# Moving the second gate's beta product and the query products from VectorE to GpSimd, and splitting the prediction's matmuls around U

## The chip, the core and the metric

The kernel runs on one core of a Trainium2 chip. The metric is the device time of one execution in microseconds, from the hardware; what is shown is the median over runs. Engines are named as in the profile: PE is TensorE's matmul, DVE is VectorE, ACT is ScalarE, POOL is GpSimd, SP is SyncE.

## The reference

The layer is an attention block with two recurrent states, followed by a routed feed-forward block. With 2 sequences of 2048 tokens, 16 heads and head size 64, each token does, per head:

```python
pred = einsum(S, kn);  r = clip(v_t - pred, -1, 1)
S = a_t * S;  S = S + b_t * kn (x) (v_t - kn.S)
o = einsum(S, q_t)
R = aR_t * R; R = R + g_t * kn (x) (r - kn.R)
o = o + einsum(R, q_t)
```

Here `b_t` is the first gate's beta and `g_t` the second gate's (it scales the whole update of R). The output is projected, normalised and added; then 64 experts (8 for each token) and one shared expert follow, with another layernorm and residual.

## The kernel before

The program has a short first stage, then `attention`, a loop over 32 chunks of 64 tokens, then a stage that runs the experts over 320 tiles of 128 tokens, then a last stage of layernorms. Each engine has its own hand-written program inside a stage; the order in the source is the order on the engine, and semaphores tie the engines together. Work for the next chunk (its projections, gates and keys) is done inside the loop body of the present one under `if front`.

In a chunk the recurrence is turned into triangular systems of 64 tokens. The tiles that matter:

- `S`, `R` are the states; `pq[:, 0]` are keys with the decay of the steps before them, `pq[:, 1]` and `rqplus` are queries times decays for the first and second state; `dec` (the tile `z`) holds the decays, `c` their inverses; `kplus`, and `c` again, are the scaled keys.
- `L_s`, `L_r` hold the triangles that are inverted: GpSimd makes beta times the strict mask (`row_coefficients`), VectorE multiplies it into PE's product in `masked`. The inverse of the 32x32 diagonal blocks is made on VectorE in 30 steps, and leaves it as `N` and `T`, two transposes that are the last things of a long unbroken VectorE run.
- PE then makes `Z` and `X` (the off-diagonal blocks), ACT and POOL put the blocks together in `inv_s` and `inv_r`. POOL copies the diagonal blocks of `inv_r`, ACT its off-diagonal ones.
- PE makes `U` = inv_s times B, then `PR` (the prediction: `pq[:,0]` with S plus `pqT` with U), `SU` (update of S), `NS` (norms of the next keys), the first part of `O`, `SD` (shared expert), `W` = inv_r times `BR`, the rest of `O`, `RU` (update of R), the next chunk's triangles `A`, `OUT` and `V`.
- VectorE makes `BR` from PR: subtract, clip, subtract `KRt`, multiply by the second gate's beta. Then come the keys of the next chunk (`k`, `c`, `kplus`, `pq`), the add into S, the query products, the add into R, and `masked`.

Matmul results go through six banks in turn (`SMALL`, in the order of `order_of_jobs`): a product waits until the one six places before it has been emptied. `O_begun` says that PE has done the first part of `O`, which reads the old query products; `queries_made` says that the new ones are there, and ACT and PE wait for it in the next chunk. POOL also issues eight scatters of rows per chunk (L391) from the third chunk on, numbers 5 to 7 of them behind `BR_ready` and `O_begun`.

## Time and profile before

| what | value |
|---|---|
| median of 3 runs | 3480.25 us (3474.77 to 3484.2) |
| the profiled execution | 3481.59 us, its span 3479.8 us |
| mean granted TensorE clock over the span | 0.889 |
| chunk loop, first to last N transpose | 110.0 to 2537.0 us |

The chunk loop takes some seventy per cent of the time, the expert stage nearly all of the rest. A busy share is an average over these stages. A line number in a row is a line of the kernel before; a pair such as `BR<-BR,beta` is the tile written and the tiles read.

### The profile page before, as it was taken

What the parts mean: (1) busy time and instruction counts of PE and PEld (TensorE: products, weight loads), DVE (VectorE), ACT (ScalarE), POOL (GpSimd) and SP (SyncE); (2) the same over time, 40 slices, a digit from 0 to 9 for tenths busy, and PEclk for the clock granted to TensorE, in tenths of its full rate; (3) what the DMA queues carried; (4) which work ended last, traced back from release to release, by engine and by line L of the source; (5) the groups of instructions that cost most, each with busy time, mean ns of one, the idle gap of its engine ahead of it and who ended that gap; (6) DMA issues with size and microseconds to landing.
All of it is one profiled execution on the core that took longest, in us unless ns stands there. A gap on an engine that the chain in (4) does not pass through costs nothing. (4 is left out here: it accounts for less than half of the span.)

```text
span 3479.8 us, 135741 instructions
## 1 busy us (share of the span) xinstructions
PE 2906.5 (84%) x56922; PEld 2571.7 (74%) x56922; DVE 2644.2 (76%) x6931; ACT 1948.5 (56%) x5132; POOL 1229.9 (35%) x1001
## 2 busy tenths in 40 slices
PE   4888888888888888889988888888855998889980
PEld 4888887878888887878888887888744776667760
...
DMA packets 193480, 240.15 MB, mean 69 GB/s; under 512 B 26738, under 2 KB 171251, under 8 KB 192115
## 3 DMA queue, kind: packets, MB, share of 16 engines
...
## 5 line engine op out<-in xcount | busy, mean ns | idle before, releaser
L391 POOL DMA_INDIRECT table<-xrow,place_i x256 | 280.4, 1095 | 764.0 <-DVE BR L866 237.8
L1475 PE MATMUL bank<-w,route 128*128 x2560 | 370.8, 288 | 35.7 <-issue 12.2
L1105 POOL COPY inv_r<-N 32x512 f32<-32x512 f32 x128 | 136.4, 1065 | 736.5 <-DVE N L842 732.5
L1475 PEld LDWEIGHTS bank<-w,route 128*128 128x128 f32 x2560 | 311.9, 192 | 104.2 <-issue 101.2
L457 DVE TENSOR_TENSOR tri<-tri,step 128x58 f32<-128x58 f32 (+13 forms) x896 | 305.5, 341 | 30.8
L456 DVE TENSOR_TENSOR step<-tri 128x58 f32<-128x58 f32 (+13 forms) x896 | 301.7, 337 | 26.4
L1490 PE MATMUL bank<-w,seen 128*128 x640 | 215.0, 418 | 52.5 <-DVE y L1563 10.2
L1551 DVE COPY to_row<-shared 128x1 int32<-128x1 int32 x228 | 35.1, 154 | 269.1 <-DMA acc<-sh_h,to_row 43.3
L1082 POOL COPY T<-L_s 32x512 f32<-32x512 f32 x64 | 38.7, 605 | 359.5 <-DVE L_s L778 358.2
L1490 PEld LDWEIGHTS bank<-w,seen 128*128 128x128 f32 x640 | 95.8, 189 | 89.2 <-issue 83.8
L589 PE MATMUL bank<-B,kT_r 64*64 64x64 f32 x2048 | 110.4, 300 | 61.4 <-DVE S L883 61.4
L783 DVE TENSOR_TENSOR_SCAN c<-restart,z 128x1024 f32<-128x1024 bf16 x62 | 158.3, 2592 | 0.0
L589 PEld LDWEIGHTS bank<-B,kT_r 64*64 64x64 f32 x2048 | 105.1, 210 | 65.6 <-DVE S L883 65.6
L948 ACT ACTIVATE z<-bank,neg_bias 128x128 f32<-128x128 f32 x496 | 137.6, 373 | 28.5 <-PE bank L604 26.1
L566 PE MATMUL bank<-S,pq 64*64 64x64 f32 x2048 | 109.6, 311 | 44.1 <-ACT U L924 44.1
L1518 ACT COPY route<-bank 128x256 f32<-128x256 f32 x320 | 119.5, 374 | 46.4 <-PE bank L1460 46.4
L1551 DVE COPY to_row<-xrow 128x1 int32<-128x1 int32 x92 | 14.2, 154 | 169.9 <-ACT shared L1527 62.6
L604 PE MATMUL bank<-xnT,wa 128*128 128x128 f32 x992 | 126.7, 289 | 18.7 <-ACT xnT L984 18.7
L969 ACT ACTIVATE S<-S,dec_end 128x64 f32<-128x64 f32 x512 | 125.8, 334 | 26.8 <-DVE S L883 26.7
L604 PEld LDWEIGHTS bank<-xnT,wa 128*128 128x128 f32 x992 | 120.8, 202 | 22.9 <-ACT xnT L984 22.8
L699 PE MATMUL bank<-Z,T 32*32 32x32 f32 x4096 | 119.8, 235 | 20.6 <-issue 20.0
L928 ACT COPY k<-bank 128x512 f32<-128x512 f32 x62 | 36.3, 585 | 179.3 <-PE bank L604 179.3
...
## 6 DMA issues: line engine op xcount, KB each, us to landing
table<-blank SPq DMA_DIRECT2D x320, 129.0 KB
...
```

The lines of the kernel that those rows point to most:

```text
L391: nc.gpsimd.indirect_dma_start(out=table, out_offset=bass.IndirectOffsetOnAxis(ap=t.place8_i[:, k:k + 1], axis=0), in_=row[:, :], in_offse ...
L456: link(nc.vector.tensor_tensor(step, s[:, 0:k, k:k + 1].broadcast_to([P, k, rest]), over(s[:, k, k + 1:Q], k), ALU.mult))
L457: link(nc.vector.tensor_tensor(s[:, 0:k, k + 1:Q], s[:, 0:k, k + 1:Q], step, ALU.add))
L589: mm = nc.tensor.matmul(ps[r, C * i:C * i + C], lhsT(r, u), rhs(r, u), start=(m == 0), stop=(m == len(pairs) - 1))
L604: mm = nc.tensor.matmul(ps[:, P * m:P * m + P], w[:, kt, P * hp:P * hp + P], t.xnT[:, kt, :], start=(kt == 0), stop=(kt == 1))
L699: mm = nc.tensor.matmul(ps[top, Q * u:Q * u + Q], t.T[top, 16 * g + u, :], t.Z[top, 16 * g + u, :], start=True, stop=True)
L783: nc.vector.tensor_tensor_scan(t.c[:, gate, :, :].rearrange("p u n -> p (u n)"), t.restart[:], t.z[:, gate, :], 0.0, ALU.mult, ALU.add).th ...
L948: ins = nc.scalar.activation(t.z[:, gate, P * hp:P * hp + P], ps[:, P * m:P * m + P], ACT.Exp, bias=t.neg_bias[:, gate, hp:hp + 1], scale= ...
L969: ins = nc.scalar.activation(state[:, u, :], state[:, u, :], ACT.Copy, scale=t.dec_end[n % 2][:, g, u:u + 1])
L1105: ins = nc.gpsimd.tensor_copy(t.inv[1][r, :, Q * (q % 2):Q * (q % 2) + Q], t.N[r, 16:32, :])
L1475: mm = nc.tensor.matmul(ps[:, begin:begin + n], t.xT_slot[i % 3][:, P * kt:P * kt + P], weights(i, 257 * kt + begin, n), start=(kt == 0), ...
L1490: nc.tensor.matmul(t.ps[y_bank[i % 2]][:, 0:256], t.hT_slot[i % 3][:, :], weights(i, 514, 256), start=True, stop=True).then_inc(t.sem["y_d ...
```

## The change

The second gate's beta no longer multiplies `BR` on VectorE. It multiplies `inv_r` on POOL: the four diagonal copies become products with beta, two more products scale the off-diagonal blocks once ACT has put them there, and the making of `L_s` and `L_r` is split around these. The two query products and the copy of the last decays go from VectorE to POOL, behind scatters 5 and 6 and the wait for `O_begun`, ahead of scatter 7. On PE the half of PR that reads S is issued before U, into its own banks, and the half that reads U after it; PR has a semaphore of its own, `PR_done`, and takes the two bank turns before U's.

```diff
@@ -72,7 +72,7 @@
     jobs = [("XT", "")] * front + two("KS") + two("a") * front + two("KR") + two("r") * front + [("BG", "")] * front
     jobs += [("RT", "")] + [("PQ", str(i)) for i in range(4)] + two("k") * front + [("RL", "")] + two("RQ")
     jobs += [("KT", f"{g}{h}") for g in range(2) for h in range(2)] + two("q") * front + [("SG", "")]
-    jobs += two("Z") + two("X") + two("U") + two("PR") + two("SU") + two("NS") * front + two("O") + [("SD", "")]
+    jobs += two("Z") + two("X") + two("PR") + two("U") + two("SU") + two("NS") * front + two("O") + [("SD", "")]
     jobs += two("W") + two("RU") + ends + [("RK", "")] * route + [("OUT", "")] + two("V") * front
     return jobs
 
...
@@ -88,7 +88,7 @@
             signalled = 0
             for p, (n, kind, name) in enumerate(mine):
                 seen[table[kind]] += 1
-                signalled += kind != "O"
+                signalled += kind not in ("O", "PR")
                 self.engine[n, name] = ("" if table is SMALL else "front_", table[kind])
                 self.done[n, name] = (p, signalled)
                 self.before[n, name] = (mine[p - banks][0], mine[p - banks][2]) if p >= banks else None
...
@@ -491,9 +491,9 @@
     return nc.scalar.activation(t.bgz[:].rearrange("p g u -> p (g u)"), ps[:, 0:32], ACT.Exp, scale=-1.0)
 
 
-def row_coefficients(nc, t, beta):
-
-    for g, h in STREAMS:
+def row_coefficients(nc, t, beta, streams):
+
+    for g, h in streams:
         half = slice(8 * h, 8 * h + 8)
         nc.gpsimd.tensor_tensor(t.L[g][:, half, :], bc(beta[:, g, half], C), over(t.neg_strict[:], 8),
                                 ALU.mult).then_inc(t.sem["coef_ready"], 1)
...
@@ -699,13 +699,15 @@
                             mm = nc.tensor.matmul(ps[top, Q * u:Q * u + Q], t.T[top, 16 * g + u, :],
                                                   t.Z[top, 16 * g + u, :], start=True, stop=True)
                     mm.then_inc(t.sem["mm_done"], 1)
+                PR = [begin(n, "PR0"), begin(n, "PR1")]
+                four(PR, odd_unit, [(lambda r, u: t.pq[r, 0, u, :], of(t.S))], last=False, whole=True)
                 pe.wait_ge(t.sem["B_ready"], n + 1)
                 wait_emptied(pe, t, o, n, "X0")
                 pe.wait_ge(t.sem["inv_s_ready"], n + 1)
                 crossed(n, "U", [(of(t.inv[0]), of(t.B))])
                 wait_emptied(pe, t, o, n, "U1")
-                crossed(n, "PR", [(lambda r, u: t.pq[r, 0, u, :], of(t.S)),
-                                  (lambda r, u: t.pqT[r, u, 0, :], of(t.U))])
+                for ins in four(PR, odd_unit, [(lambda r, u: t.pqT[r, u, 0, :], of(t.U))], first=False, whole=True):
+                    ins.then_inc(t.sem["PR_done"], 1)
                 for h in range(2):
                     units(n, f"SU{h}", h, [(of(t.kT[0]), of(t.U))])
                 if front:
...
@@ -720,7 +722,6 @@
                 ps = begin(n, "SD")
                 wait_emptied(pe, t, o, n, "SG")
                 shared_down(nc, t, ps).then_inc(t.sem["front_mm"], 1)
-                wait_emptied(pe, t, o, n, "X1")
                 pe.wait_ge(t.sem["inv_r_ready"], n + 1)
                 pe.wait_ge(t.sem["BR_ready"], 2 * n + 2)
                 crossed(n, "W", [(of(t.inv[1]), of(t.BR))])
...
@@ -856,14 +857,14 @@
                     route_best(nc, t, link)
                 for h in range(2):
                     r, rest = even_odd(t.BR, h), even_odd(t.KRt, h)
-                    ps = mm(n, f"PR{h}")
+                    dve.wait_ge(t.sem["PR_done"], 2 * n + h + 1)
+                    ps = o.bank(t, n, f"PR{h}")
                     nc.vector.tensor_tensor(r, even_odd(t.V, h), blk(ps[:, :]),
                                             ALU.subtract).then_inc(t.sem["dve_emptied"], 1)
                     wait_emptied(dve, t, o, n, f"PR{h}")
                     link(nc.vector.tensor_scalar(r, r, -1.0, 1.0, ALU.max, ALU.min))
                     wait_emptied(dve, t, o, n, "KR1")
-                    link(nc.vector.tensor_tensor(r, r, rest, ALU.subtract))
-                    nc.vector.tensor_tensor(r, r, bc(t.beta[n % 2][:, 1, h:16:2], C), ALU.mult).then_inc(t.sem["BR_ready"], 1)
+                    nc.vector.tensor_tensor(r, r, rest, ALU.subtract).then_inc(t.sem["BR_ready"], 1)
                 if route:
                     dve.wait_ge(t.sem["sel_ready"], o.base("sel_ready", n + 1))
                     route_weights(nc, t, link, t.xrow[n % 2])
...
@@ -882,11 +883,6 @@
                     ps = mm(n, f"SU{h}")
                     nc.vector.tensor_tensor(t.S[:, half[h], :], blk(ps[:, :]), t.S[:, half[h], :],
                                             ALU.add).then_inc(t.sem["dve_emptied"], 1)
-                if front:
-                    wait_emptied(dve, t, o, n, "q1")
-                    nc.vector.tensor_tensor(t.pq[:, 1, :, :], t.q[:], t.dec[:, 0, :, :], ALU.mult)
-                    nc.vector.tensor_tensor(t.rqplus[:], t.q[:], t.dec[:, 1, :, :], ALU.mult)
-                    nc.vector.tensor_copy(t.dec_end[(n + 1) % 2][:], t.dec[:, :, :, C - 1]).then_inc(t.sem["queries_made"], 1)
                 for h in range(2):
                     ps = mm(n, f"RU{h}")
                     nc.vector.tensor_tensor(t.R[:, half[h], :], blk(ps[:, :]), t.R[:, half[h], :],
...
@@ -1102,22 +1098,41 @@
                 pool.wait_ge(t.sem["N_ready"], n + 1)
                 for q in range(4):
                     r = slice(Q * q, Q * q + Q)
-                    ins = nc.gpsimd.tensor_copy(t.inv[1][r, :, Q * (q % 2):Q * (q % 2) + Q], t.N[r, 16:32, :])
+                    ins = nc.gpsimd.tensor_tensor(t.inv[1][r, :, Q * (q % 2):Q * (q % 2) + Q], t.N[r, 16:32, :],
+                                                  bc(t.beta[n % 2][r, 1, :], Q), ALU.mult)
+                ins.then_inc(t.sem["inv_r_begun"], 1)
+                pool.wait_ge(t.sem["inv_r_begun"], n + 1)
+                if front:
+                    wait_done(pool, t, o, n, "Z1")
+                    pool.wait_ge(t.sem["beta_ready"], n + 1)
+                    row_coefficients(nc, t, t.beta[(n + 1) % 2], STREAMS[0:2])
+                    pool.wait_ge(t.sem["coef_ready"], o.base("coef_ready", n) + 2)
+                wait_emptied(pool, t, o, n, "X1")
+                for j in range(2):
+                    r = slice(C * j, C * j + Q)
+                    ins = nc.gpsimd.tensor_tensor(t.inv[1][r, :, Q:2 * Q], t.inv[1][r, :, Q:2 * Q],
+                                                  bc(t.beta[n % 2][r, 1, :], Q), ALU.mult)
                 ins.then_inc(t.sem["inv_r_ready"], 1)
                 pool.wait_ge(t.sem["inv_r_ready"], n + 1)
                 if front:
-                    wait_done(pool, t, o, n, "Z1")
-                    pool.wait_ge(t.sem["beta_ready"], n + 1)
-                    row_coefficients(nc, t, t.beta[(n + 1) % 2])
+                    row_coefficients(nc, t, t.beta[(n + 1) % 2], STREAMS[2:4])
                 if n >= 2:
                     pool.wait_ge(t.sem["BR_ready"], 2 * n + 1)
                     scatter_row(nc, t, d.table, t.xrow[(n - 1) % 2], 5)
                     pool.wait_ge(t.sem["BR_ready"], 2 * n + 2)
                     scatter_row(nc, t, d.table, t.xrow[(n - 1) % 2], 6)
+                if front:
+                    pool.wait_ge(t.sem["dec_ready"], 2 * n + 2)
+                    wait_emptied(pool, t, o, n, "q1")
                     pool.wait_ge(t.sem["O_begun"], n + 1)
+                    nc.gpsimd.tensor_tensor(t.pq[:, 1, :, :], t.q[:], t.dec[:, 0, :, :], ALU.mult)
+                    nc.gpsimd.tensor_tensor(t.rqplus[:], t.q[:], t.dec[:, 1, :, :], ALU.mult)
+                    nc.gpsimd.tensor_copy(t.dec_end[(n + 1) % 2][:], t.dec[:, :, :, C - 1]).then_inc(t.sem["queries_made"], 1)
+                if n >= 2:
                     scatter_row(nc, t, d.table, t.xrow[(n - 1) % 2], 7)
                     wait_scattered(pool, t, n - 1)
                 if front:
+                    pool.wait_ge(t.sem["queries_made"], o.base("queries_made", n) + 1)
                     diagonal(n)
 
 
...
@@ -1169,7 +1184,7 @@
                                     t.k[:].rearrange("p u n -> p (u n)"), ALU.mult).then_inc(t.sem["keys_squared"], 1)
             pool.wait_ge(t.sem["beta_ready"], 1)
             pool.wait_ge(t.sem["late_loaded"], 16 * len(late))
-            row_coefficients(nc, t, t.beta[0])
+            row_coefficients(nc, t, t.beta[0], STREAMS)
             pool.wait_ge(t.sem["key_ready"], 1)
             for g in range(2):
                 pool.wait_ge(t.sem["dec_ready"], g + 1)
```

On VectorE, in one chunk, this is what stood from the scaling of the next keys by their norms to the triangles (`x2` is a pair of equal instructions):

```order
L873 TENSOR_TENSOR k<-k,tri 128x1024
L876 TENSOR_TENSOR c<-k,c 128x2048
L877 TENSOR_TENSOR kplus<-k,z 128x2048
L878 TENSOR_TENSOR pq<-k,z 128x16x63
L879 COPY pq<-k 128x16
L883 TENSOR_TENSOR S<-bank,S 128x512 x2
L887 TENSOR_TENSOR pq<-q,z 128x1024
L888 TENSOR_TENSOR rqplus<-q,z 128x1024
L889 COPY dec_end<-z 128x32
L892 TENSOR_TENSOR R<-bank,R 128x512 x2
L778 TENSOR_TENSOR L_s<-bank,L_s 128x8x64 x2
```

and this is what stands there now, with the lines' new numbers:

```order
L874 TENSOR_TENSOR k<-k,tri 128x1024
L877 TENSOR_TENSOR c<-k,c 128x2048
L878 TENSOR_TENSOR kplus<-k,z 128x2048
L879 TENSOR_TENSOR pq<-k,z 128x16x63
L880 COPY pq<-k 128x16
L884 TENSOR_TENSOR S<-bank,S 128x512 x2
L888 TENSOR_TENSOR R<-bank,R 128x512 x2
L779 TENSOR_TENSOR L_s<-bank,L_s 128x8x64 x2
```

The three instructions on queries and decays are gone; keys, S, R and the triangles keep their order. Ahead of this piece the two products `BR<-BR,beta` are gone as well.

On POOL one chunk, from the transposed inverse to the copies of the triangles' diagonals, read before:

```order
L1105 COPY inv_r<-N 32x16x32 x4
L498 TENSOR_TENSOR L_s<-beta,neg_strict 128x512 x2
L498 TENSOR_TENSOR L_r<-beta,neg_strict 128x512 x2
L391 DMA table<-xrow,place_i 41088x258 x3
L1082 COPY T<-L_s 32x512 x2
L1082 COPY T<-L_r 32x512 x2
```

and reads now:

```order
L1101 TENSOR_TENSOR inv_r<-N,beta 32x16x32 x4
L498 TENSOR_TENSOR L_s<-beta,neg_strict 128x512 x2
L1113 TENSOR_TENSOR inv_r<-inv_r,beta 32x16x32 x2
L498 TENSOR_TENSOR L_r<-beta,neg_strict 128x512 x2
L391 DMA table<-xrow,place_i 41088x258 x2
L1128 TENSOR_TENSOR pq<-q,z 128x1024
L1129 TENSOR_TENSOR rqplus<-q,z 128x1024
L1130 COPY dec_end<-z 128x32
L391 DMA table<-xrow,place_i 41088x258
L1078 COPY T<-L_s 32x512 x2
L1078 COPY T<-L_r 32x512 x2
```

The query products stand between scatters 6 and 7, and the diagonal copies `T<-L_s` come behind them.

On PE the piece from the off-diagonal blocks to the update of S, where PR alternated between its two sources in sixteen groups, began before with

```order
L699 MATMUL bank<-Z,T 32x32 x64
L566 MATMUL bank<-B,inv_s 64x64 x32
L566 MATMUL bank<-S,pq 64x64 x4
L566 MATMUL bank<-U,pqT 64x64 x4
L566 MATMUL bank<-S,pq 64x64 x4
```

and reads now

```order
L699 MATMUL bank<-Z,T 32x32 x64
L566 MATMUL bank<-S,pq 64x64 x32
L566 MATMUL bank<-B,inv_s 64x64 x32
L566 MATMUL bank<-U,pqT 64x64 x32
L589 MATMUL bank<-U,kT_s 64x64 x32
```

The S half of PR stands whole ahead of U, the U half whole behind it.

## Rows read from the trace of the kernel before

**Rows 1.** Page, part 1: busy us, share of the span, instructions of each engine
```profile
PE 2906.5 (84%) x56922; PEld 2571.7 (74%) x56922; DVE 2644.2 (76%) x6931; ACT 1948.5 (56%) x5132; POOL 1229.9 (35%) x1001
```
**Rows 2.** One line's instructions: the transpose that ends each chunk's triangle inversion
```profile
L842 DVE STREAM_TRANSPOSE N<-tri x32: 2007/2070/2101, 110.0 to 2537.0; 128x1024 f32<-128x1024 f32 x32
```
**Rows 3.** Timeline of one chunk, DVE: start, duration, line, operation, idle before, releaser
```profile
1222.01 0.69 DVE L860 TENSOR_TENSOR BR<-V,bank 128x512 f32<-128x512 f32 x1 [1.91 <-PE bank L566]
...
1223.92 0.69 DVE L866 TENSOR_TENSOR BR<-BR,beta 128x512 f32<-128x512 f32 x1
...
1229.86 1.23 DVE L873 TENSOR_TENSOR k<-k,tri 128x1024 f32<-128x1024 f32 x1 [1.96 <-ACT tri L472]
1231.12 2.29 DVE L876 TENSOR_TENSOR c<-k,c 128x2048 f32<-128x2048 f32 x1
1233.33 2.28 DVE L877 TENSOR_TENSOR kplus<-k,z 128x2048 f32<-128x2048 f32 x1
1235.53 1.20 DVE L878 TENSOR_TENSOR pq<-k,z 128x1008 f32<-128x1008 f32 x1
...
1236.74 1.28 DVE L883 TENSOR_TENSOR S<-bank,S 128x512 f32<-128x512 f32 x2
1237.93 1.22 DVE L887 TENSOR_TENSOR pq<-q,z 128x1024 f32<-128x1024 f32 x1
1239.07 1.22 DVE L888 TENSOR_TENSOR rqplus<-q,z 128x1024 f32<-128x1024 f32 x1
...
1240.31 1.41 DVE L892 TENSOR_TENSOR R<-bank,R 128x512 f32<-128x512 f32 x2
1242.16 1.29 DVE L778 TENSOR_TENSOR L_s<-bank,L_s 128x512 f32<-128x512 f32 x2 [0.45 <-PE bank L566]
```
**Rows 4.** Timeline of the same chunk, PE
```profile
1214.79 2.27 PE L566 MATMUL bank<-B,inv_s 64*64 64x64 f32 x64
1218.29 0.49 PE L566 MATMUL bank<-S,pq 64*64 64x64 f32 x8 [1.23 <-ACT U L924]
...
1221.75 3.09 PE L589 MATMUL bank<-U,kT_s 64*64 64x64 f32 x64
...
1232.08 1.16 PE L566 MATMUL bank<-BR,inv_r 64*64 64x64 f32 x64
...
1237.48 3.39 PE L589 MATMUL bank<-B,kT_r 64*64 64x64 f32 x62 [1.91 <-DVE S L883]
```
**Rows 5.** Timeline of the same chunk, POOL
```profile
1208.32 4.44 POOL L1105 COPY inv_r<-N 32x512 f32<-32x512 f32 x4 [21.38 <-DVE N L842]
1212.85 3.89 POOL L498 TENSOR_TENSOR L_s<-beta,neg_strict 128x512 f32<-128x512 f32 x2
1216.71 2.04 POOL L498 TENSOR_TENSOR L_r<-beta,neg_strict 128x512 f32<-128x512 f32 x2
...
1231.37 2.90 POOL L391 DMA_INDIRECT table<-xrow,place_i  x1 [3.00 <-PE bank L566]
1243.61 1.25 POOL L1082 COPY T<-L_s 32x512 f32<-32x512 f32 x2 [9.34 <-DVE L_s L778]
```
**Rows 6.** Timeline of the last stage, DVE and POOL, two places
```profile
3432.40 1.22 DVE L1598 TENSOR_TENSOR sum<-sum 128x1024 f32<-128x1024 f32 x1
3432.57 3.25 POOL L1637 TENSOR_TENSOR row<-sum,row 128x1024 f32<-128x1024 f32 x1 [11.66 <-DVE sum L1609]
...
3447.71 2.34 POOL L1637 TENSOR_TENSOR row<-sum,row 128x1024 f32<-128x1024 f32 x1 [1.79 <-DVE sum L1609]
3448.72 2.42 DVE L1598 TENSOR_TENSOR sum<-sum 128x1024 f32<-128x1024 f32 x1 [1.08 <-DMA row<-x_rows]
```
**Rows 7.** Windows, same chunk: length; busy PE, PEld, DVE, ACT, POOL; granted clock; DMA; GB/s
```profile
1237.70:1241.10 3.40, 3.40 (x82) 3.40 (x82) 3.37 (x6) 3.40 (x16) 0.00 (x0) 0.50 0.12 30
```
**Rows 8.** Timeline of three chunks later, DVE
```profile
1470.52 1.28 DVE L883 TENSOR_TENSOR S<-bank,S 128x512 f32<-128x512 f32 x2
...
1475.29 1.28 DVE L778 TENSOR_TENSOR L_s<-bank,L_s 128x512 f32<-128x512 f32 x2
```

2 lines of the change are left out of this document (1 added, 1 removed).

## The prediction

> **What bounds the kernel now.** I read the page first: VectorE is busy 76% of the span and PE 84%, POOL 35% [rows 1]. These shares mix stages, so I read the chunk loop alone. Its transposes of N start at 110.0 and, 32 of them, at 2537.0 [rows 2], so a chunk takes (2537.0 - 110.0)/31 = 78.3 us. Then I read the timelines of one middle chunk, engine by engine, looking for the places where an engine stands idle and who lets it go on.
>
> VectorE runs without a pause from the triangles `L_s` at 1242.16 until the next chunk's prediction PR. It pauses three times: 1.91 us for PR, 1.96 us for ACT's key norms, 0.45 us for PE's triangle products [rows 3]. PE pauses 1.23 us for ACT's copy of U and 1.91 us for VectorE's add into S, which empties the bank that RU needs [rows 4]. So in the part of the chunk that the change touches, the chain that sets the end is: U, copy of U, PR, SU and the norms on PE; norms on ACT; then on VectorE `k`, `c`, `kplus`, `pq`, S (1229.86 to 1238.02); then RU and the triangle products on PE; then `L_s` on VectorE. What matters is which of the edits lies on that chain.
>
> **Beta off VectorE.** Two products of 0.69 us leave [rows 3]. They stand before the 1.96 us wait for the norms, and these come from PE and ACT. W, which reads BR, starts at 1232.08, long after BR is made, with no idle time before it [rows 3, 4]. So VectorE waits 1.4 us longer for the norms: price 0. On POOL four copies become products and two more are added. The nearest rows: the four copies took 4.44 us, two 128x512 products 2.04 us where nothing was in the way and 3.89 us where a scan was [rows 5]. The six products cost thus 6 x 1.02 = 6.1 us to 6 x 1.94 = 11.7 us, in place of 4.44. L_s and L_r cost 5.9 us as before. POOL started at 1208.32; even at the upper end it is through at 1208.3 + 11.7 + 5.9 = 1225.9, and `inv_r` is ready before that, ahead of W at 1232.08. Products on POOL also hold up some of VectorE's short routing operations; the cover is the 1.91 us before PR plus the norm wait of 1.96 + 1.4 us, together 5.3 us. If that cover were gone, each microsecond over it would be one on the chain, 31 us in all.
>
> **PR in two halves.** PE goes from X straight into U, with no idle time [rows 4], so there is no gap for the first half to fill. The whole of PR took from 1218.29 to 1221.75, 3.46 us; half is 1.73 us. U and its copy end 1.73 us later, and 1.73 us less remains behind them: PR ends where it did. Price 0. If the copy's start hid a little of ACT's own work it could be 0.1 us better; if the groups run worse apart than interleaved, worse by as little.
>
> **Query products off VectorE.** 1.22 + 1.22 us and a short copy leave, standing between the add into S and the add into R: from 1237.93 to 1240.31, 2.38 us [rows 3]. It looks like 74 us in 31 chunks. But RU starts at 1237.48, off the first half of S, and takes 3.39 us; the triangles follow it on PE, and `L_s` waited 0.45 us for PE even with the query products in place [rows 3, 4]. VectorE would only wait longer. Price 0 while PE is this slow there. The granted clock in that stretch is 0.50, 1.2 GHz of the two levels [rows 7]. Where it was full, the distance from S to `L_s` was 1475.29 - 1470.52 = 4.77 us against 5.42 us, with no wait [rows 3, 8]; only in such chunks can the removal pay.
>
> **Query products onto POOL.** This is the term that decides. POOL may start when `O_begun` arrives. Before, scatter 7 waited for just that and started at 1231.37 [rows 5]; the query products start there now, 0.25 us after VectorE began `c` at 1231.12. VectorE then does three products with both operands in SBUF: `c`, `kplus`, `pq` [rows 3]. The last stage shows what becomes of two such products on the two engines. POOL's product, started 0.17 us after VectorE's, took 3.25 us and ended 2.20 us after the end of VectorE's; with nothing in the way it took 2.34 us, the same shape as a query product. VectorE's, started 1.01 us into POOL's, took 2.42 in place of 1.22 us and ended 1.08 us after POOL's end, so 0.14 us of its duration passed before it was held up [rows 6]. They take turns, a whole instruction at a time, and each waits for the other.
>
> Turn by turn. `c` ends at 1233.41. POOL's first product has waited since 1231.4, ends at 1233.41 + 2.20 = 1235.61. `kplus` ends at 1235.61 + 2.28 - 0.14 = 1237.75 in place of 1235.61: 2.14 us late. POOL's second, waiting by then, ends at 1239.95; `pq` ends at 1239.95 + 1.20 - 0.14 = 1241.01 in place of 1236.73: 4.28 us late. If POOL comes first, before `c`, two of the three are held up all the same. The adds into S have one operand in PSUM, and a copy on POOL beside the same kind of instruction at 1243.61 took 0.63 us each, so they add nothing. So the add into S is 4.28 us late, on the chain: RU, triangles and `L_s` move by as much, PE standing idle 1.91 + 4.28 = 6.2 us. 31 chunks prepare a next one: 31 x 4.28 = +133 us. Bounds: 0, if POOL's products always yield and run behind `pq`; 2.14 us per chunk if only one finds itself in the way; above, 4.28 and what the clock costs on top (below). I take 4.28, since both directions of the turn have their row. The Trainium skill (Perfetto Trace Analysis, Optimizing Scalar/DVE Operations) says that offloading from a saturated DVE to GpSimd may make sense, but that the two share an SBUF read port, so it might not help. By that sentence alone this term would be 0 or better, and the rows say that it costs.
>
> What is behind POOL's products: scatter 7, then the copies into T. The queries end near 1240.2, `L_s` now comes near 1246.4, so there is room for the scatter (2.90 us at most in these rows) before the copies [rows 5]: price 0.
>
> **Sum.** 3481.6 (the profiled execution) + 133 = 3614.6. That execution is 1.3 us over the median of the runs shown, so 3613 for the median.
>
> **Rivals.** (1) One turn only. Speaks for it: the second product may find `pq` already begun. 31 x 2.14 = 66 us: 3547. A PE clock that recovers earlier, since the S half of PR joins X and U in one unbroken stretch, gives similar: half of SU's 3.09 us would be 1.5 us per chunk, 48 us off the 133: 3565. Against: in the middle chunk nothing but the copy of U separated PR from U before either.
> (2) The clock costs on top. PE idles 6.2 us before RU. RU then runs 3.39 us at the low level, but the triangles ran mostly at full clock, and would slow too: about 2.2 us more at the very most (their share of 5.42 - 3.39 = 2.0 us, doubled), so up to 62 us: 3675; half of that, 3644, is likelier. The Trainium skill (TensorE: Matmul & The Clock Gate, HAM oscillation) says that recurring waits throttle the engine again each time. By that rule this is what would come; the trace agrees as far as the 0.50 in the stretch after a wait of 1.91 us.
> (3) No change: POOL's products yield to VectorE's, which are queued back to back, and run beside the adds. All moved work was hidden or becomes hidden: 3480. Against: POOL's product in the last stage did not yield to what VectorE had next [rows 6], but VectorE's next there was no such product.
> (4) Faster: as (3), and PE, less broken, keeps its full clock over RU. Then VectorE sets `L_s`, and the removed 2.38 us and the 0.65 us between 5.42 and 4.77 pay, less what PE needs: at most 3.03 x 31 = 94 us, I take half: 3433. It decides from the point where the turns cost less than 3.03 us per chunk, so one turn at 2.14 us would already leave it a little faster if the clock held. Against: the low clock stands after the very wait that would have to shrink.
>
> **Chances.** Two full turns, 0.68; (1) 0.12; (2) 0.10; (3) 0.05; (4) 0.05. The range runs from 3545, below both forms of (1), to 3655, above the likelier half of (2). 0.3%, some 10 us, is about what a measurement of this kernel can tell from no change. Faster by more 0.05, within it 0.05, slower 0.90. The forecast's own range, given its case, is 3590 to 3640.
>
> **What the changed profile would show.** Each turn: `kplus` and `pq` at about 4.4 and 3.3 us in place of 2.28 and 1.20, and POOL's two products at over 4 us each in place of 2.33. `k` waits some 3.4 us for the norms. RU waits over 6 us for S. R and `L_s` wait for PE, by more than 0.45 us. The U wait on PE stays near 1.23 us and PR ends at the same distance from N. The forecast is wrong if `kplus` and `pq` keep their durations, or if the long run of VectorE from `L_s` to N changes its length.

## The result and the profile after

The changed kernel takes 3595.97 us (median of 4 runs, 3594.27 to 3598.03) against 3481.61 us before (3474.77 to 3484.2): a ratio of 1.0332, 95% interval 1.0314 to 1.0350. It is 3.3% slower. Its profiled execution took 3595.86 us, with a span of 3594.1 us and a mean granted TensorE clock of 0.889, as before. Comparisons leave disturbed runs out.

Part 1 of its page (busy us, share, instructions), which answers to [rows 1]:

```profile
PE 2875.6 (80%) x56922; PEld 2555.4 (71%) x56922; DVE 2756.1 (77%) x6774; ACT 1951.3 (54%) x5132; POOL 1605.9 (45%) x1158
```

VectorE has 157 instructions less and is busy 112 us more. That is the first thing to see: what was left on it became longer. The transpose that ends each inversion, answering to [rows 2]:

```profile
L843 DVE STREAM_TRANSPOSE N<-tri x32: 2017/2080/2106, 112.2 to 2655.9; 128x1024 f32<-128x1024 f32 x32
```

A chunk takes (2655.9 - 112.2)/31 = 82.05 us in place of 78.29. 31 x 3.76 = 116.7 us, against 114.3 us between the two profiled executions: the loss is in the chunk loop. Timeline of one chunk on DVE (its N starts at 1102.49), answering to [rows 3]:

```profile
1118.43 1.00 DVE L339 TENSOR_TENSOR route<-route 128x64 f32<-128x64 f32 x1
1119.35 0.67 DVE L862 TENSOR_TENSOR BR<-V,bank 128x512 f32<-128x512 f32 x1
...
1123.86 1.23 DVE L874 TENSOR_TENSOR k<-k,tri 128x1024 f32<-128x1024 f32 x1
1125.12 2.29 DVE L877 TENSOR_TENSOR c<-k,c 128x2048 f32<-128x2048 f32 x1
1127.33 4.44 DVE L878 TENSOR_TENSOR kplus<-k,z 128x2048 f32<-128x2048 f32 x1
1131.69 3.34 DVE L879 TENSOR_TENSOR pq<-k,z 128x1008 f32<-128x1008 f32 x1
...
1135.08 1.27 DVE L884 TENSOR_TENSOR S<-bank,S 128x512 f32<-128x512 f32 x2
1137.83 0.69 DVE L888 TENSOR_TENSOR R<-bank,R 128x512 f32<-128x512 f32 x1 [1.48 <-PE bank L589]
1139.54 0.69 DVE L888 TENSOR_TENSOR R<-bank,R 128x512 f32<-128x512 f32 x1 [1.02 <-PE bank L589]
1141.31 1.29 DVE L779 TENSOR_TENSOR L_s<-bank,L_s 128x512 f32<-128x512 f32 x2 [1.08 <-PE bank L566]
```

POOL in the same chunk, answering to [rows 5]:

```profile
1104.77 8.12 POOL L1101 TENSOR_TENSOR inv_r<-N,beta 32x512 f32<-32x512 f32 x4 [21.84 <-DVE N L843]
1112.96 2.05 POOL L498 TENSOR_TENSOR L_s<-beta,neg_strict 128x512 f32<-128x512 f32 x2
1115.09 2.14 POOL L1113 TENSOR_TENSOR inv_r<-inv_r,beta 32x512 f32<-32x512 f32 x2
1117.30 2.04 POOL L498 TENSOR_TENSOR L_r<-beta,neg_strict 128x512 f32<-128x512 f32 x2
...
1126.89 2.73 POOL L1128 TENSOR_TENSOR pq<-q,z 128x1024 f32<-128x1024 f32 x1 [2.64 <-PE bank L566]
1129.57 4.40 POOL L1129 TENSOR_TENSOR rqplus<-q,z 128x1024 f32<-128x1024 f32 x1
1133.92 1.21 POOL L1130 COPY dec_end<-z 128x32 f32<-128x32 f32 x1
```

Read the two timelines against each other. `c` (from 1125.12, 2.29 us) ends at 1127.41, as long as in before. POOL's first product ends at 1129.62, `kplus` at 1131.77, POOL's second at 1133.97, `pq` at 1135.03. The ends alternate, 2.21, 2.15, 2.20 and 1.06 us apart, about what each instruction takes alone, less the overlap with the one before. So each duration in the rows holds the other engine's turn too. From the start of `c` to the add into S it is 1135.08 - 1125.12 = 9.96 us, where it was 1236.74 - 1231.12 = 5.62 us [rows 3].

PE in the same chunk, answering to [rows 4]:

```profile
1113.12 1.57 PE L566 MATMUL bank<-B,inv_s 64*64 64x64 f32 x64
1115.82 1.17 PE L566 MATMUL bank<-U,pqT 64*64 64x64 f32 x63 [1.12 <-ACT U L920]
...
1116.86 1.98 PE L589 MATMUL bank<-U,kT_s 64*64 64x64 f32 x62
...
1135.81 3.57 PE L589 MATMUL bank<-B,kT_r 64*64 64x64 f32 x62 [4.63 <-DVE S L884]
```

RU waits 4.63 us for S, where it waited 1.91. But SU (`U,kT_s`) takes 1.98 us where it took 3.09: the clock is up again by then. Windows (length; busy PE, PEld, DVE, ACT, POOL; clock; DMA; GB/s) show where it rises. First two of the chunk of [rows 4], which hold its U and PR:

```profile
1214.30:1217.70 3.40, 2.75 (x84) 2.40 (x78) 3.23 (x15) 2.79 (x6) 3.40 (x3) 0.50 0.03 7
1217.70:1221.10 3.40, 2.81 (x104) 2.82 (x108) 2.06 (x12) 3.37 (x5) 1.04 (x2) 0.50 0.00 0
```

Then three of the chunk above, in after, the last of which holds the U half of PR:

```profile
1106.70:1110.00 3.30, 2.62 (x94) 2.40 (x90) 3.30 (x2) 3.19 (x7) 3.18 (x3) 0.58 0.18 56
1110.00:1113.50 3.50, 3.50 (x131) 3.44 (x131) 3.43 (x5) 3.02 (x5) 3.42 (x2) 0.50 0.02 5
1113.50:1117.00 3.50, 2.38 (x133) 2.24 (x127) 3.19 (x17) 2.45 (x5) 3.36 (x4) 0.92 0.02 5
```

Three groups of before that the rows ahead of the prediction don't have (busy us, mean ns | idle before them in the whole run, and which instruction ended it):

```profile
L860 DVE TENSOR_TENSOR BR<-V,bank 128x512 f32<-128x512 f32 x64 | 43.8, 684 | 69.8 <-PE bank L566 69.8
...
L873 DVE TENSOR_TENSOR k<-k,tri 128x1024 f32<-128x1024 f32 x31 | 38.0, 1225 | 48.4 <-ACT tri L472 48.4
...
L330 DVE TENSOR_TENSOR route<-route,groups 128x64 f32<-128x64 f32 x32 | 7.2, 226 | 1.1
```

and the groups of after:

```profile
L1129 POOL TENSOR_TENSOR rqplus<-q,z 128x1024 f32<-128x1024 f32 x31 | 130.6, 4212 | 0.0
L878 DVE TENSOR_TENSOR kplus<-k,z 128x2048 f32<-128x2048 f32 x31 | 126.8, 4090 | 0.0
L1128 POOL TENSOR_TENSOR pq<-q,z 128x1024 f32<-128x1024 f32 x31 | 112.1, 3617 | 82.9 <-PE bank L566 82.9
L879 DVE TENSOR_TENSOR pq<-k,z 128x1008 f32<-128x1008 f32 x31 | 95.2, 3070 | 0.0
L888 DVE TENSOR_TENSOR R<-bank,R 128x512 f32<-128x512 f32 x64 | 44.3, 691 | 79.2 <-PE bank L589 79.2
L862 DVE TENSOR_TENSOR BR<-V,bank 128x512 f32<-128x512 f32 x64 | 43.3, 677 | 9.5 <-PE bank L566 9.5
L779 DVE TENSOR_TENSOR L_s<-bank,L_s 128x512 f32<-128x512 f32 x64 | 41.2, 686 | 48.5 <-PE bank L566 48.5
L874 DVE TENSOR_TENSOR k<-k,tri 128x1024 f32<-128x1024 f32 x31 | 38.0, 1225 | 22.6 <-ACT tri L472 21.5 <-DVE xrow L347 0.2
L330 DVE TENSOR_TENSOR route<-route,groups 128x64 f32<-128x64 f32 x32 | 33.1, 1033 | 1.1
```

For the account I cut each chunk at five starts on VectorE: N, `k`, the first add into S, `L_s`, and the transpose of `tri` from T that opens the next inversion (tri in the table). Below are the means over 31 chunks in us, worked out from the trace of each kernel's profiled execution, with the time at half clock in three of the stretches. The large gain of this case stands in the column N-k, the large loss in k-S:

```
kernel             chunk   N-k   k-S   S-L  L-tri tri-N | half clock N-k, k-tri, tri-N
before             78.29 23.30  6.90  5.58  7.72 34.80 | 12.33 4.18 1.72
after              82.05 21.91 11.20  6.00  7.74 35.20 |  7.93 7.82 3.38
e1_split_pr        77.34 22.74  6.87  5.31  7.74 34.68 |  9.80 3.30 2.53
e2_queries         83.14 23.32 11.12  5.88  7.73 35.09 | 11.78 9.25 3.37
e3_beta            78.34 23.49  6.87  5.54  7.73 34.72 | 12.88 4.18 2.31
e4_pr_beta         77.61 22.72  6.87  5.21  7.92 34.89 |  9.80 2.64 2.90
e5_behind_s        77.84 22.17  6.87  4.59  8.89 35.32 |  8.59 1.32 3.80
e6_halves          80.27 22.08  9.97  5.45  7.74 35.04 |  8.48 4.62 2.26
e7_pr_behind_s     78.05 21.50  6.87  5.12  8.91 35.64 |  7.05 3.08 5.77
e8_repeat          78.73 23.42  6.88  5.21  7.73 35.50 |  7.93 2.42 3.80
e9_filler          77.13 22.10  6.88  5.24  7.74 35.16 |  7.82 2.53 2.76
e10_two_fillers    77.07 22.14  6.89  5.11  7.96 34.98 |  7.71 0.11 2.26
e11_ahead_of_a     78.70 21.99  6.87  5.38  8.90 35.56 |  8.04 3.52 3.67
e12_three_fillers  76.72 22.04  6.89  4.99  7.94 34.86 |  8.04 0.11 1.69
```

After against before, us per chunk: -1.39 +4.30 +0.42 +0.02 +0.40 = +3.75, which is the 3.76 up to rounding.

A row is one execution, and it need not be the median one. That of e7_pr_behind_s took 3467.52 us, the shortest of its 12, 18 us (0.6 a chunk) under their median; that of e6_halves is 13 us under its median, those of e2_queries 7 and of e5_behind_s and e12_three_fillers 5 us. Differences of a few tenths of a us per chunk between two rows are no surer than that.

Nearly all of what differs in tri-N has one place: `pqT<-bank,pq_mask`, where VectorE waits for PE's products of keys and queries. The prediction read this stretch as unbroken; in before it has this wait of 12.7 us in all. In the order of that wait, which is also the order of tri-N: e1_split_pr 8.0 us (34.68), before 12.7 (34.80), e12_three_fillers 14.8, e10_two_fillers 17.7, e9_filler 22.5, after 22.6 (35.20), e5_behind_s 26.6, e8_repeat 31.4, e11_ahead_of_a 31.8, e7_pr_behind_s 34.2 (35.64). Two of these rows (us in all, times, longest), of e1_split_pr and of e7_pr_behind_s:

```profile
DVE pqT L826 <- PE bank L661: 8.0, 28, 1.2
...
DVE pqT L826 <- PE bank L661: 34.2, 80, 1.0
```

### The profile page after: what moved, and what is told of

It reads as the page before. It is cut to its first block and busy times, and to the rows that moved or that the text cites. A ratio compares the mean times of both kernels' runs of the same rounds, so it can differ in the third digit from the quotient of the medians.

```text
span 3594.1 us, 135835 instructions
## 1 busy us (share of the span) xinstructions
PE 2875.6 (80%) x56922; PEld 2555.4 (71%) x56922; DVE 2756.1 (77%) x6774; ACT 1951.3 (54%) x5132; POOL 1605.9 (45%) x1158
## 5 line engine op out<-in xcount | busy, mean ns | idle before, releaser
L1101 POOL TENSOR_TENSOR inv_r<-N,beta 32x512 f32<-32x512 f32 x128 | 250.5, 1957 | 752.5 <-DVE N L843 746.9
L391 POOL DMA_INDIRECT table<-xrow,place_i x256 | 254.9, 996 | 548.9 <-issue 142.0
L604 PE MATMUL bank<-xnT,wa 128*128 128x128 f32 x992 | 138.5, 306 | 57.7 <-ACT xnT L980 57.7
L784 DVE TENSOR_TENSOR_SCAN c<-restart,z 128x1024 f32<-128x1024 bf16 x62 | 180.3, 2946 | 0.0
L604 PEld LDWEIGHTS bank<-xnT,wa 128*128 128x128 f32 x992 | 132.6, 219 | 62.0 <-ACT xnT L980 62.0
L1128 POOL TENSOR_TENSOR pq<-q,z 128x1024 f32<-128x1024 f32 x31 | 112.1, 3617 | 82.9 <-PE bank L566 82.9
L661 PE MATMUL bank<-pq,c 64*64 64x128 f32 x2048 | 147.8, 310 | 0.0
L661 PEld LDWEIGHTS bank<-pq,c 64*64 64x64 f32 x2048 | 140.1, 159 | 6.2 <-issue 6.2
```

The lines of the kernel that those rows point to most:

```text
L391: nc.gpsimd.indirect_dma_start(out=table, out_offset=bass.IndirectOffsetOnAxis(ap=t.place8_i[:, k:k + 1], axis=0), in_=row[:, :], in_offse ...
L604: mm = nc.tensor.matmul(ps[:, P * m:P * m + P], w[:, kt, P * hp:P * hp + P], t.xnT[:, kt, :], start=(kt == 0), stop=(kt == 1))
L661: mm = nc.tensor.matmul(ps[r, 2 * C * m:2 * C * m + 2 * C], t.kminus[0][r, u, :], t.pq[r, :, u, :], start=True, stop=True)
L784: nc.vector.tensor_tensor_scan(t.c[:, gate, :, :].rearrange("p u n -> p (u n)"), t.restart[:], t.z[:, gate, :], 0.0, ALU.mult, ALU.add).th ...
L1101: ins = nc.gpsimd.tensor_tensor(t.inv[1][r, :, Q * (q % 2):Q * (q % 2) + Q], t.N[r, 16:32, :], bc(t.beta[n % 2][r, 1, :], Q), ALU.mult)
```

## The experiments: each part alone

### e1_split_pr: the split of PR alone

Before with only the split, its main lines:

```diff
-    jobs += two("Z") + two("X") + two("U") + two("PR") + two("SU") ...
+    jobs += two("Z") + two("X") + two("PR") + two("U") + two("SU") ...
...
+                PR = [begin(n, "PR0"), begin(n, "PR1")]
+                four(PR, odd_unit, [(lambda r, u: t.pq[r, 0, u, :], of(t.S))], last=False, whole=True)
...
-                crossed(n, "PR", [(lambda r, u: t.pq[r, 0, u, :], of(t.S)),
-                                  (lambda r, u: t.pqT[r, u, 0, :], of(t.U))])
+                for ins in four(PR, odd_unit, [(lambda r, u: t.pqT[r, u, 0, :], of(t.U))], first=False, whole=True):
+                    ins.then_inc(t.sem["PR_done"], 1)
```

> The kernel before with one edit: the S half of PR ahead of U, the U half behind it. Theory (the split gives PE an unbroken stretch ahead of the copy of U, so its clock is back earlier): the half clock in the part from N to k falls from 12.3 us per chunk towards the 7.9 of the changed kernel, k starts some 1.5 us earlier after N; part is given back by a low clock later in the chunk (0.8 us in the changed kernel), so 0.6 to 1.4 us per chunk, 3440 to 3465 us. Rival (the earlier clock came from the longer chunk, not from the split): N to k stays at 23.3 us and the time within 0.3% of before.

Measured: 3455.84 against 3482.25 us, 0.9914 (0.9891 to 0.9937). The split is not free, it gains. N-k is 0.56 us shorter and S-L 0.27, with 2.5 us less half clock in N-k.

### e2_queries: the query products alone

Before with only the queries' three lines moved:

```diff
DVE, between the adds into S and R:
-                if front:
-                    wait_emptied(dve, t, o, n, "q1")
-                    nc.vector.tensor_tensor(t.pq[:, 1, :, :], t.q[:], t.dec[:, 0, :, :], ALU.mult)
-                    nc.vector.tensor_tensor(t.rqplus[:], t.q[:], t.dec[:, 1, :, :], ALU.mult)
...
POOL, behind the wait for O_begun and ahead of scatter 7:
+                    nc.gpsimd.tensor_tensor(t.pq[:, 1, :, :], t.q[:], t.dec[:, 0, :, :], ALU.mult)
+                    nc.gpsimd.tensor_tensor(t.rqplus[:], t.q[:], t.dec[:, 1, :, :], ALU.mult)
...
```

> The kernel before with one edit: the query products on GpSimd, between scatters 6 and 7. Theory (two turns at the shared port): k to S grows from 6.90 to 11.2 us, N to k stays at 23.3, so 31 x 4.3 = 133 us and some clock on top: 3610 to 3640 us. Rival (the stall belongs to the three edits together, or to GpSimd's beta products that keep it late): k to S stays under 9 us, under 3550 us.

Measured: 3636.06 against 3482.25 us, 1.0439 (1.0418 to 1.0460), as expected. k-S is 11.12 us (+4.22), most of the 4.85 us by which a chunk is longer; S-L has 0.30 and tri-N 0.29 of it. Half clock from `k` to the transpose goes from 4.18 to 9.25 us, so the clock's own cost comes with this part.

### e3_beta: beta on POOL alone

After, with the edits of e1_split_pr and e2_queries undone. What is left of the change, its main lines:

```diff
-                    nc.vector.tensor_tensor(r, r, bc(t.beta[n % 2][:, 1, h:16:2], C), ALU.mult).then_inc(t.sem["BR_ready"], 1)
...
-                    ins = nc.gpsimd.tensor_copy(t.inv[1][r, :, Q * (q % 2):Q * (q % 2) + Q], t.N[r, 16:32, :])
+                    ins = nc.gpsimd.tensor_tensor(t.inv[1][r, :, Q * (q % 2):Q * (q % 2) + Q], t.N[r, 16:32, :],
+                                                  bc(t.beta[n % 2][r, 1, :], Q), ALU.mult)
...
```

> The kernel before with one edit: the second gate's beta on GpSimd, in inv_r. Theory: the beta products hold up the scans and routing operations of VectorE, but these end before the wait for the norms does, so the time stays within 0.3% (3471 to 3492 us), and k waits for the norms no longer than before. Rival (the hold-ups reach the chain): slower by over 0.5%.

Measured: 3483.42 us, 1.0006 (0.9995 to 1.0017), no difference. The wait for the norms did grow, though the expectation had it no longer than before: 73.1 us in all ahead of `k` against 48.4, while that for PR ahead of BR shrank from 69.8 to 15.2. The three parts alone make -0.86% +4.39% +0.06% = +3.59%, together they make +3.32%.

### e4_pr_beta: after, with the queries back on VectorE

The edit of e2_queries undone in after:

```diff
+                    nc.vector.tensor_tensor(t.pq[:, 1, :, :], t.q[:], t.dec[:, 0, :, :], ALU.mult)
+                    nc.vector.tensor_tensor(t.rqplus[:], t.q[:], t.dec[:, 1, :, :], ALU.mult)
...
-                    nc.gpsimd.tensor_tensor(t.pq[:, 1, :, :], t.q[:], t.dec[:, 0, :, :], ALU.mult)
-                    nc.gpsimd.tensor_tensor(t.rqplus[:], t.q[:], t.dec[:, 1, :, :], ALU.mult)
...
```

> The changed kernel with the query products and decay copy put back on VectorE, so the split of PR and the beta edit alone. Theory: the whole loss was the query products; k to S is back at 6.9 us, N to k stays near 21.9, so 3440 to 3470 us, faster than before. Rival (beta's hold-ups eat what the earlier clock gives): within 0.3% of before.

Measured: 3457.01 us, 0.9917 (0.9894 to 0.9940), and 77.61 us a chunk against after's 82.05. The move of the queries costs 4.44 us a chunk in after, and beta gives nothing on top of the split. But N-k is 22.72 us here, as in e1_split_pr, and not after's 21.91: the last 0.8 us of after's gain ahead of `k`, with 1.9 us less half clock, come only when the queries move too. Why is open.

## The experiments: is it the turns?

### e5_behind_s: POOL's query products start when S is done

After, with one more wait for POOL, so that `c`, `kplus` and `pq` are through:

```diff
                     pool.wait_ge(t.sem["O_begun"], n + 1)
+                    wait_emptied(pool, t, o, n, "SU0")
                     nc.gpsimd.tensor_tensor(t.pq[:, 1, :, :], ...
```

> The changed kernel with one more wait: GpSimd starts the query products when the first add into S is done, not when O_begun comes. Same work on the same engines. Theory (turns with c, kplus and pq): k to S is back at 6.9 us, kplus and pq at 2.28 and 1.20 us, GpSimd's products near 2.33 us each beside adds that read one operand from PSUM; 3425 to 3460 us. Rival (the products cost VectorE wherever they run): the stall moves to the adds into R and the triangles, and the time stays over 3540 us.

Measured: 3469.24 against 3479.20 us, 0.9975 (0.9951 to 0.9999); its ten runs lie between 3451.8 and 3489.1 us. DVE of one chunk:

```profile
995.07 2.29 DVE L878 TENSOR_TENSOR kplus<-k,z 128x2048 f32<-128x2048 f32 x1
997.27 1.20 DVE L879 TENSOR_TENSOR pq<-k,z 128x1008 f32<-128x1008 f32 x1
...
1002.79 0.69 DVE L888 TENSOR_TENSOR R<-bank,R 128x512 f32<-128x512 f32 x1 [0.86 <-PE bank L589]
1003.79 1.29 DVE L779 TENSOR_TENSOR L_s<-bank,L_s 128x512 f32<-128x512 f32 x2 [0.31 <-PE bank L566]
1005.80 1.29 DVE L779 TENSOR_TENSOR L_r<-bank,L_r 128x512 f32<-128x512 f32 x2 [0.72 <-PE bank L566]
...
1008.70 0.56 DVE L357 TENSOR_TENSOR route<-route 128x64 f32<-128x64 f32 x1
...
1009.43 0.52 DVE L360 TENSOR_TENSOR route<-route 128x64 f32<-128x64 f32 x1
```

and POOL:

```profile
999.34 2.37 POOL L1129 TENSOR_TENSOR pq<-q,z 128x1024 f32<-128x1024 f32 x1 [9.88 <-DVE S L884]
1001.67 2.36 POOL L1130 TENSOR_TENSOR rqplus<-q,z 128x1024 f32<-128x1024 f32 x1
...
1007.27 1.25 POOL L1078 COPY T<-L_s 32x512 f32<-32x512 f32 x2 [1.88 <-DVE L_r L779]
```

The same work on the same engines, started later: all four products have their own lengths, and k-S is 6.87 us. So it is their running beside `c`, `kplus` and `pq` that costs. The second add into R, one of whose inputs is in PSUM, lies wholly beside POOL's second product and takes 0.69 us, as after's adds into R do, which have no product beside them. The Trainium skill (SBUF — State Buffer, Who interferes with whom) says just this: a VectorE instruction with two inputs in SBUF contends with a GpSimd one that reads SBUF, one with at most one such input, outside the two-port modes, does not. The trace agrees for these products and adds. That one input in SBUF is not by itself safe is seen in e6_halves, where a VectorE copy is held up.

It was to come to 3425 to 3460 us and did not. S-L is 1.0 us shorter than before, but L-tri 1.17 us longer and tri-N 0.52. `L_r` waits 0.72 us here, 0.70 in the mean, where it hardly waits in before; and POOL's copies into T now lie beside the routing products, of which L357 takes 0.56 us and L360 0.52, 0.23 each in before. The trace gives PE's product as what `L_r` waited for. By the modelled end of its matmuls that product was done about 1.2 us earlier, but its semaphore came only at 1005.78; why so late stays open. The longer tri-N is the wait at `pqT`, 26.6 us in all against 12.7.

### e6_halves: half as long an instruction, half as long a turn

After, each of POOL's two products cut in two, of 128x512:

```diff
-                    nc.gpsimd.tensor_tensor(t.pq[:, 1, :, :], t.q[:], t.dec[:, 0, :, :], ALU.mult)
-                    nc.gpsimd.tensor_tensor(t.rqplus[:], t.q[:], t.dec[:, 1, :, :], ALU.mult)
+                    for h in range(2):
+                        nc.gpsimd.tensor_tensor(t.pq[:, 1, half[h], :], t.q[:, half[h], :], t.dec[:, 0, half[h], :], ALU.mult)
+                    for h in range(2):
+                        nc.gpsimd.tensor_tensor(t.rqplus[:, half[h], :], t.q[:, half[h], :], t.dec[:, 1, half[h], :], ALU.mult)
```

> The changed kernel with each of GpSimd's two query products issued as two of half the length, same data. Theory (one whole instruction of GpSimd goes in between two of VectorE): still only two turns fall between c, kplus and pq, of half the length, so the stall is some 2 us instead of 4.3: k to S near 8.9 us, about 3596 - 31 x 2.2 = 3530 us. Rival (the port's rate is shared, the loss goes by the amount of data): no change from 3596 us.

Measured: 3560.57 us, 1.0239 (1.0218 to 1.0260). DVE of one chunk:

```profile
1188.30 3.35 DVE L878 TENSOR_TENSOR kplus<-k,z 128x2048 f32<-128x2048 f32 x1
1191.58 2.26 DVE L879 TENSOR_TENSOR pq<-k,z 128x1008 f32<-128x1008 f32 x1
1193.76 1.23 DVE L880 COPY pq<-k 128x16 f32<-128x16 f32 x1
```

and POOL:

```profile
1186.43 6.34 POOL L1129 TENSOR_TENSOR pq<-q,z 128x512 f32<-128x512 f32 x2 [3.69 <-PE bank L566]
1192.74 3.45 POOL L1131 TENSOR_TENSOR rqplus<-q,z 128x512 f32<-128x512 f32 x2
```

`kplus`, `pq` and the copy behind them are each some 1.06 us longer, one half product, where `kplus` and `pq` were 2.15 us longer in after. k-S is 9.97 us on average, 3.07 more than before, where 8.9 was expected: I had counted two instructions that can be held up, and there is a third, a copy of 16 values a partition, 0.18 us in e5_behind_s and 1.23 here. The price of a turn goes with the length of POOL's instruction. The number of turns is bounded by the instructions that either engine has: with whole products POOL has two. After's trace shows this in all 31 chunks: exactly two of `c`, `kplus`, `pq` and the copy are held up for a whole turn, `c` and `kplus` in 4 chunks, `kplus` and `pq` in 22, `pq` and the copy (2.3 us for its 16 values) in 5. Where POOL starts decides which two, not how many. The rate-shared rival, no change from 3596 us, is out by 35 us.

### e7_pr_behind_s: the split, and the queries behind S, with beta left on VectorE

e1_split_pr with the edit of e2_queries and e5_behind_s's wait:

```diff
+                    wait_emptied(pool, t, o, n, "SU0")
+                    nc.gpsimd.tensor_tensor(t.pq[:, 1, :, :], t.q[:], t.dec[:, 0, :, :], ALU.mult)
```

> The kernel before with the split of PR and with the query products on GpSimd behind the first add into S; beta stays on VectorE. Theory (PE sets the triangles, so VectorE's freed 2.4 us buy little, and what is bought is given back on PE in the second part): within 15 us of the split alone, 3440 to 3470 us; S to L shorter by 0.6 us, L to the next stage or the stretch up to N longer by about as much. Rival (the removal pays once the port is free, and the run with beta was held back by beta's products): 3425 us or less.

Measured: 3485.88 us (3467.5 to 3497.8) against 3479.44, 1.0028 (1.0014 to 1.0041). Both expectations missed: the best N-k of all (21.50) and none of the turns, but L-tri +1.19 and tri-N +0.84 us, and the median run is another 0.6 us a chunk longer than this profile. So beta on POOL is not what spoils e5_behind_s; queries behind S are: beside the split alone (0.9914) they cost over 1%. In one chunk of this kernel PE stands idle for 2.13 us ahead of the projections `a` of the next chunk, and then takes 6.61 us for their 32 records at the low clock. That became a suspect (e11_ahead_of_a).

## The experiments: what the split gains by

Two explanations were left for the 0.9 us per chunk of e1_split_pr: less work behind U, or a clock that rises earlier, since PE works longer without a break before U's copy. The extra products in the kernels below are thrown away; they only keep PE at work. A product of the source is two records in the trace, and the products here are counted as in the source.

### e8_repeat: the S half ahead of U, and all of PR behind it

e1_split_pr with the S half as extra work whose result is overwritten:

```diff
-                four(PR, odd_unit, [(... t.pq[r, 0, u, :], of(t.S))], last=False, whole=True)
+                four(PR, odd_unit, [(... t.pq[r, 0, u, :], of(t.S))], whole=True)
-                for ins in four(PR, odd_unit, [(... of(t.U))], first=False, whole=True):
+                for ins in four(PR, odd_unit, [(... of(t.S)), (... of(t.U))]):
```

> The kernel before with the S half of PR issued ahead of U as extra work, and the whole of PR again behind U, so nothing is taken from behind the copy of U. Theory (what the split brings is the clock): the half clock from N to k falls as in the split alone (9.8 us per chunk against 12.3), which pays back most of the 1.7 us per chunk of extra work: 3470 to 3500 us. Rival (the split pays since less is left behind the copy): the extra work costs its full 31 x 1.7 = 54 us, about 3535 us.

Measured: 3490.77 us, 1.0036 (1.0022 to 1.0050). N-k is 23.42 us, about as before (23.30), though PE does 32 more products in it: half clock there falls from 12.33 to 7.93 us and pays for them. So work ahead of U brings the clock up earlier, with nothing taken from behind the copy of U. That this is all that e1_split_pr gains by is likely, not shown: the extra work itself keeps the clock up more than the split does (7.93 us of half clock against 9.80), so the two kernels do not differ by the tail alone.

### e9_filler, e10_two_fillers, e12_three_fillers: work in PE's waits

e9 is e1_split_pr with 12 small products between U and the rest of PR, where PE waits for ACT's copy. e10 adds 32 ahead of RU, where PE waits for the add into S. e12 adds four ahead of `a`.

```diff
e9, behind U:
+                spare = begin(n, "SU0")
+                for u in range(6):
+                    for j in range(2):
+                        r = slice(C * j, C * j + C)
+                        nc.tensor.matmul(spare[r, 0:C], t.kT[0][r, u, :], t.B[r, u, :], start=True, stop=True)
...
e10, behind the rest of O, into W0's emptied bank: the same with range(16) and t.U
...
e12, ahead of the wait for XT:
+                    spare = begin(n, "a0")
+                    for i in range(4):
+                        nc.tensor.matmul(spare[:, 0:P], t.wa[:, 0, 0:P], t.wa[:, 0, P:2 * P], start=True, stop=True)
```

> The split of PR alone, with 12 extra small products per chunk on PE between U and the second half of PR, where PE otherwise waits some 1.2 us for the copy of U; their result is thrown away. Theory (the clock comes back late in the chunks where that pause falls badly): the half clock from N to k falls below 9.8 us per chunk, nearly all chunks take the 75 to 76 us that a third of them take with the split alone, 3380 to 3430 us. Rival (the pause has no part in it): as the split alone, 3456 us, or later by the products' own time.

> The kernel with the split of PR and extra small products between U and the second half of PR, with 32 more between the last part of O and RU, where PE waits 1.9 us for the add into S; their result is thrown away. Theory (each pause of PE costs clock): the half clock from k to the end of the triangles' stage falls from 2.5 towards 1 us per chunk, S to L from 5.24 to under 5.0 us, 3420 to 3440 us. Rival (the low clock moves on to the next pause and costs the same there): 3443 us, with more half clock in the stretch up to N.

> The kernel with the split of PR and extra small products at two pauses of PE (behind U, ahead of RU), with 4 more ahead of the projections a. Theory: the half clock up to N falls from 2.3 us per chunk, a few tenths of a us per chunk, 3425 to 3437 us; the pause there is only 0.4 us in the mean, so if the extra products reach into busy time it is 3437 to 3445 us. Rival (nothing is left to gain from the clock there): 3437 us as without them.

Measured: e9 3443.03 us, 0.9896 (0.9874 to 0.9918); e10 3437.21 us, 0.9882 (0.9865 to 0.9900); e12 3434.64 us, 0.9883 (0.9864 to 0.9901). A window of e10 in the stretch of RU, where before has 0.50 [rows 7]:

```profile
1143.20:1146.60 3.40, 2.87 (x124) 2.79 (x115) 3.40 (x6) 2.26 (x7) 0.00 (x0) 1.00 0.54 163
```

e9 lowers half clock in N-k from 9.80 to 7.82 us and N-k by 0.64 us, but tri-N gives 0.48 of it back, at `pqT`; the 3380 to 3430 that I expected are missed, and its interval overlaps that of e1_split_pr (0.9891 to 0.9937), so a gain of its own is not shown. e10 takes half clock in k-tri from 2.53 to 0.11 us, and gains 0.13 us in S-L, which L-tri gives back (+0.22): in S-L of e9 VectorE waits for PE only 0.37 us a chunk, so there is little to gain. e12 has tri-N at 34.86 us; its interval lies on that of e10. Both beat the two kernels of this case by some 1.2% and 4.4%.

### e11_ahead_of_a: seven extra products ahead of `a`, in e7_pr_behind_s

```diff
+                    spare = begin(n, "a0")
+                    for i in range(7):
+                        nc.tensor.matmul(spare[:, 0:P], t.wa[:, 0, 0:P], t.wa[:, 0, P:2 * P], start=True, stop=True)
```

> The kernel with the split of PR and the query products on GpSimd behind the first add into S, with 7 extra products on PE just ahead of the projections a, where PE waits 2.1 us in most chunks for the next tokens; their result is thrown away. Theory (PE got ahead, stood idle and lost its clock there, so a took 6.6 us instead of 3.8): a is back near 4 us, the half clock in the stretch up to N falls from 5.8 to under 3 us per chunk, tri to N from 35.6 to under 35.0 us, 3435 to 3465 us. Rival (the stretch grew by GpSimd's collisions or VectorE's own work): 3486 us, tri to N stays at 35.6 us.

Measured: 3486.64 us, 1.0018 (1.0004 to 1.0032). One product of `a` has a median of 421 ns in e7_pr_behind_s:

```profile
L604 PE MATMUL bank<-xnT,wa x992: 274/421/582, 78.2 to 2428.7; 128*128 128x128 f32 x199
```

and 275 ns in e11_ahead_of_a:

```profile
L604 PE MATMUL bank<-xnT,wa x992: 274/275/580, 77.8 to 2449.3; 128*128 128x128 f32 x199
```

The clock is mended for `a`, the half clock in tri-N falls from 5.77 to 3.67 us (not under 3), and tri-N stays at 35.56 us. The theory fell: the slower `a` is not what makes the inversion's stretch longer when the queries run behind S. The traces say where the time goes: VectorE waits at `pqT` for PE, 31.8 us in all here and 34.2 in e7_pr_behind_s against 8.0 in e1_split_pr, 0.85 of the 0.96 us by which tri-N of e7_pr_behind_s is longer than that of e1_split_pr. Why PE is late with these products is open.

## Why the prediction was right, step by step

- **Query products onto POOL, +4.28 us a chunk.** Right in mechanism and size: k-S grew by 4.30 us, and `kplus` took 4.44 and `pq` 3.34 us in the middle chunk. e2_queries, e5_behind_s and e6_halves show the cause by doing it alone, moving it in time, and halving it. The start of POOL's products was misread: they were released 1.77 us after `c` began and not 0.25, so the first took 2.73 us rather than over 4 (mean 3.62). It cost nothing, since two turns come about either way, as the prediction had said of an earlier start.
- **The other signs.** R and `L_s` waited for PE by over 1 us, and the U wait stayed (1.12 us), as forecast. Three signs did not come. `k` did not wait 3.4 us for the norms: in the middle chunk not at all, and 22.6 us in all. RU waited 4.63 us and not over 6: S came 4.34 us later behind the start of `k`, but PE was ready for RU 1.61 us later too; it had stood 1.20 us for VectorE's `BR` ahead of the first part of `O`. And PR ended 14.6 us behind N, not at the 15.9 of before.
- **PR in two halves, price 0.** This step failed, as far as anything did. "U and its copy end 1.73 us later, and PR ends where it did" holds at one clock. PE does the same products, but in another order about its wait, and the clock rises earlier. The split alone (e1_split_pr) lowers half clock in N-k from 12.33 to 9.80 us, gives 0.56 us there and 0.95 over the chunk, 0.86% of the time. In after N-k is 1.39 us shorter, with 7.93 us of half clock; the 0.8 us beyond the split's own came only together with the moved queries (e4_pr_beta against after). The second form of rival (1) had the mechanism, an earlier clock on top of both turns at 48 us off; measured are 31 x 1.39 = 43 us. It had a share of 0.12 with one turn; that nothing but the copy of U separated PR from U before either, its argument against, did not keep the clock from rising earlier.
- **Beta off VectorE, price 0.** Right for the time (e3_beta). There VectorE waits 0.8 us a chunk longer for the norms, of the 1.4 forecast. The rest of the cover of 5.3 us went to short products that POOL's held up: the wait ahead of BR fell from 69.8 to 15.2 us in all. In after, with the split, both waits shrank, ahead of `k` from 48.4 to 22.6 us and ahead of BR from 69.8 to 9.5. In the middle chunk POOL's six products took 8.12 + 2.14 = 10.3 us, within the bounds, and `L_s` and `L_r` 4.1, so POOL was through at 1119.3. But the short products beside them grew, L330 from 0.23 to 1.03 us on average, and VectorE, never idle from N on, came to BR only at 1119.35. The cover was mostly used up.
- **Query products off VectorE, price 0.** Right for this kernel: R waited 79.2 us in all for PE and `L_s` 48.5. That their removal is worth nothing anywhere is not shown. Behind S (e5_behind_s against e4_pr_beta, e7_pr_behind_s against e1_split_pr) S-L is 0.62 and 0.19 us shorter, but L-tri and tri-N take it back.
- **The clock costs on top (rival 2).** Seen at a small size: half clock from `k` to the transpose rose from 4.18 to 7.82 us, and S-L by 0.42. With tri-N, longer by 0.40, it is 25 us in place of the 62 at most (whose "2.2 us" should read 2.0). Of the 0.40 us 0.3 are VectorE's wait at `pqT` (12.7 to 22.6 us in all); that this one is the clock's doing is not shown, and e11_ahead_of_a, where half clock fell and the wait stayed, speaks against it. It is also the second sign by which the prediction would call itself wrong, a changed length of the run from `L_s` to N: the mechanism of the large term held, but this stretch was misread as unbroken. Of waits like that for S the Trainium skill (TensorE: Matmul & The Clock Gate, HAM oscillation) says that recurring waits, of a kernel that waits for DMA, throttle the engine each time; the trace agrees with the direction, after waits for VectorE.
- **Rivals 3 and 4** fell with `kplus` at 4.44 us. POOL's product did not yield to VectorE's queued ones.

The sum by what was measured: 31 x (4.30 + 0.42 + 0.40 + 0.02 - 1.39) = 116 us over 3481.6, less some 2 us outside the loop: 3595.9. The forecast of 3613 is 17 us high: it lacks the -43 us ahead of `k` and the +25 us behind S. That it came so near is in part luck: these two errors have opposite signs.
